# Normalisation statistics in four groups of eight tiles, with three of the roots on GpSimd, and parts and middle parts at other places in the order

## What is computed

```
xn = layernorm(x)                        # (x - mean) / sqrt(var + 1e-5)
Q, K, V = relu(xn @ W + b)               # 16 heads of 8 features
s  = softmax(causal(Q K^T / sqrt(8)), keys of live rows) V, masked by live queries
s  = gamma * norm(s + xn) + beta
# the other branch, on xn:
xa = (norm(xn) * ln_scale + ln_bias) @ attn_w.T + attn_b + xn
h  = gelu(xa @ w1[expert] + b1);  eo = h @ w2[expert] + b2
g  = silu(gelu(eo @ next_w.T + next_b))
out = x + s * g
```

## Time and profile before

| | us |
|---|---|
| three runs | 449.56, 454.50, 458.17 |
| median of the runs | 454.5 |
| the profiled execution, its own time | 449.74 |
| span of the profiled execution (first to last instruction) | 447.7 |
| mean granted TensorE clock, share of full | 0.977 |

### The profile page before, as it was taken

The page is one execution under the profiler, slowest core; times in us unless marked ns, Lnnn a source line. Parts: engine busy times, 40 slices in busy tenths (PEclk is TensorE's granted clock), DMA queues, the critical chain, the costliest instruction groups (busy, mean ns, idle before and its releaser), DMA issues.

```text
span 447.7 us, 9695 instructions
## 1 busy us (share of the span) xinstructions
PE 382.7 (85%) x3541; PEld 249.0 (56%) x3541; DVE 370.2 (83%) x865; ACT 289.1 (65%) x580; POOL 173.5 (39%) x448
## 2 busy tenths in 40 slices
PE   0046997899999996999999999999999999999950
PEld 0023863477777873466656665666566566656420
DVE  5899698968988523989899998999998998989427
ACT  0115742388888971377877877878778778778740
POOL 8333004211011122102147456556374474565591
PEclk9996899999999999999999999999999999999995
DMA  8930300386553428332332423332423324240000
GB/s 232 295 91 1 89 13 0 102 145 154 154 153 91 131 52 175 57 94 78 92 78 68 127 60 112 83 92 77 131 63 93 100 76 118 62 110 27 3 25 23
DMA packets 31413, 41.72 MB, mean 93 GB/s; under 512 B 5910, under 2 KB 23686, under 8 KB 31366
## 3 DMA queue, kind: packets, MB, share of 16 engines
q1 hardware_dynamic: 31206, 41.08, 35.3%
q0 software_dynamic: 160, 0.03, 0.1%
HBM read 26.43 MB, written 11.02 MB: 84 GB/s over the span
## 4 chain that ended last, share of the span: by engine, by line
PE 44%; DVE 13%; issue 2%; ACT 1%; POOL 1%; DVEq 0%; ACTq 0%; POOLq 0%
PE banks L1154 15%; PE banks L1137 8%; DVE mx L953 8%; PE banks L1117 8%; PE banks L1119 5%; PE banks L1139 5%; DVE stats L998 2%; PE banks L1164 2%; DVE res L992 1%; ACT pt L1072 1%; PE banks L1126 0%; DVE res L979 0%; DVE res L982 0%; DVE mixed L983 0%; DVE aggr L1002 0%
## 5 line engine op out<-in xcount | busy, mean ns | idle before, releaser
L953 DVE TENSOR_REDUCE mx<-banks 128x1 f32<-128x512 f32 (+3 forms) x352 | 200.1, 636 | 19.9 <-PE banks L1119 18.2
L1072 ACT ACTIVATE pt<-banks 128x512 f32<-128x512 f32 x320 | 169.2, 601 | 44.2 <-PE banks L1139 36.8
L1154 PE MATMUL banks<-pt,vg 128*18 128x512 f32 (+3 forms) x1024 | 81.4, 436 | 0.7 <-ACT pt L1072 0.7
L1117 PE MATMUL banks<-k_own,q_own 76*128 76x384 bf16 (+2 forms) x192 | 48.4, 274 | 5.5 <-DVE mx L953 2.7
L1117 PE MATMUL banks<-w_room 76*128 76x384 bf16 (+2 forms) x192 | 48.1, 274 | 3.3 <-DVE mx L953 3.3
L844 POOL TENSOR_SCALAR mneg<-mx 128x16 f32<-128x16 f32 x32 | 8.1, 253 | 108.1 <-DVE mx L953 106.9
L1137 PE MATMUL banks<-w_room 76*128 76x384 bf16 (+2 forms) x192 | 47.5, 275 | 0.9 <-ACT pt L1072 0.5
L1154 PEld LDWEIGHTS banks<-pt,vg 128*18 128x18 f32 x1024 | 23.7, 97 | 43.8 <-issue 33.4
L1137 PE MATMUL banks<-q_own,k_own 76*128 76x384 bf16 (+2 forms) x192 | 47.8, 274 | 0.0
L1119 PE MATMUL banks<-k_own,q_own 124*128 124x128 bf16 x256 | 44.0, 219 | 0.0
L1119 PE MATMUL banks<-w_room 124*128 124x128 bf16 x256 | 43.8, 219 | 0.0
(11 more groups left out here) (177 smaller groups left out, 746.7 us busy)
## 6 DMA issues: line engine op xcount, KB each, us to landing
k_scratch<-parts SPq DMA_DIRECT2D x40, 128.0 KB, 2.4
k_own<-k_scratch SPq DMA_DIRECT2D x48, 96.0 KB
w_room<-k_scratch SPq DMA_DIRECT2D x48, 96.0 KB
q_scratch<-parts SPq DMA_DIRECT2D x24, 128.0 KB, 2.4
q_own<-q_scratch SPq DMA_DIRECT2D x32, 96.0 KB
w_room<-q_scratch SPq DMA_DIRECT2D x32, 96.0 KB
w_room<-in_w_dram SPq DMA_DIRECT2D x1, 2048.0 KB, 9.3
q_own<-q_scratch SPq DMA_DIRECT2D x16, 112.0 KB
```

The costliest lines, as they stand in the source:

```text
L953: dve.tensor_reduce(mx[:, u % 2, heads[0]:heads[-1] + 1, q], banks[:, S0 + slots[0] % SLOTS, 0:w * len(heads)].rearrange("p (h k) -> p h k ...
L1072: act.activation(pt[:, T * j:T * j + T], banks[:, bank(), :], ACT.Exp, scale=SCALE).then_inc(exp_done, 1)
L1117: mm(o[:, 0:w - P], qx[by][0:LIVE, g, h, P * q:P * q + P], kx[by][0:LIVE, g, h, 0:w - P], start=True, stop=True)
L1154: ins = mm(banks[32 * h:32 * h + VP, OT, P * k:T], vg[:, g, k, h, :], pt[:, KPLACE[k, h]:KPLACE[k, h] + n], start=(k == 0 and g % 2 == 0), ...
```

## The change

The x rows are still loaded in two pieces (`LOADS`), but the statistics are made in four groups of eight tiles, one group for two sequences. The roots of group 0 stay on VectorE. For groups 1 to 3 VectorE makes means, variances and the seed (`statistics`, which increments `first_seeds`), GpSimd does the three Newton steps and the correction of the root (`first_roots`, 27 instructions) and, at a later place, its halves (`root_halves`, 4 instructions, then `roots_ready`), and VectorE takes the reciprocal (`inverses`) ahead of the quotients. `halves` splits by a product with 4097 in place of a mask of bits, since GpSimd does it in float32. The second roots are done for each of the four groups. On VectorE `sums(i)` stands right behind `quotients(i)`, then `lows(i - 2)`, then `rests(i - 1)`, and the statistics of groups 2 and 3 come behind these at i = 2 and i = 4; those of group 1 ahead of `quotients(1)`. On ScalarE both middle parts (`mids(i)`) move from between the gelus of h to behind the gelu of g in `gelu_out(i)`, for the last sequence behind its eight gelus; sequence 0 has another order, and a gelu of one element stands at the start. On TensorE the 68 held products at i = 1 go, and 22 stand at the start, behind waits for `bias_ready` and `seeds_ready`.

```diff
-GROUPS = ((0, 2 * TB), (2 * TB, NT - 2 * TB))
+LOADS = ((0, 2 * TB), (2 * TB, NT - 2 * TB))
+GROUPS = tuple((2 * TB * k, 2 * TB) for k in range(B // 2))
...
-HELD = (28, 40)
+HELD = 22
...
+                def halves(x, hi, lo, u, w):
+                    link(pool.tensor_scalar(u, x, 4097.0, None, ALU.mult))
+                    link(tt(w, u, x, ALU.subtract))
+                    link(tt(hi, u, w, ALU.subtract))
+                    link(tt(lo, x, hi, ALU.subtract))
+                def first_roots(tok, group):
+                    at = slice(group[0], group[0] + group[1])
+                    a_, y_, t_, u_, s_, sh_, sl_, rem_ = (v[:, at] for v in (a, y, t, t3, s, sh, sl, rem))
+                    pool.wait_ge(first_seeds, tok.next(first_seeds))
+                    for _ in range(3):
+                        link(tt(t_, y_, y_, ALU.mult))
+                        link(tt(t_, t_, a_, ALU.mult))
+                        link(pool.tensor_scalar(t_, t_, -0.5, 1.5, ALU.mult, ALU.add))
+                        link(tt(y_, y_, t_, ALU.mult))
+                    link(tt(s_, a_, y_, ALU.mult))
+                    halves(s_, sh_, sl_, t_, u_)
+                    link(tt(t_, sh_, sh_, ALU.mult))
+                    link(tt(rem_, a_, t_, ALU.subtract))
+                    link(tt(t_, sh_, sl_, ALU.mult))
+                    link(tt(t_, t_, t_, ALU.add))
+                    link(tt(rem_, rem_, t_, ALU.subtract))
+                    link(tt(t_, sl_, sl_, ALU.mult))
+                    link(tt(rem_, rem_, t_, ALU.subtract))
+                    link(tt(t_, rem_, y_, ALU.mult))
+                    link(pool.tensor_scalar(t_, t_, 0.5, None, ALU.mult))
+                    link(tt(s_, s_, t_, ALU.add))
+                def root_halves(group):
+                    at = slice(group[0], group[0] + group[1])
+                    halves(s[:, at], sh[:, at], sl[:, at], t[:, at], t3[:, at])
+                    pool.sem_inc(roots_ready, 1)
...
                 for i in range(B):
-                    if i == 0:
-                        second_roots(tok, GROUPS[0])
-                    if i == 2:
-                        second_roots(tok, GROUPS[1])
+                    if i % 2 == 0:
+                        second_roots(tok, GROUPS[i // 2])
                     totals(tok, i)
+                    if i % 2 == 1 and i + 1 < B:
+                        root_halves(GROUPS[(i + 1) // 2])
+                    if i % 2 == 0 and i + 2 < B:
+                        first_roots(tok, GROUPS[i // 2 + 1])
...
+                def inverses(tok, group):
+                    at = slice(group[0], group[0] + group[1])
+                    dve.wait_ge(roots_ready, tok.next(roots_ready))
+                    link(dve.reciprocal(r[:, at], s[:, at]))
+                    link(dve.tensor_scalar(nr[:, at], r[:, at], -1.0, None, ALU.mult))
...
+                def statistics(group):
+                    at = slice(group[0], group[0] + group[1])
+                    means(group)
+                    variances(group)
+                    rsqrt_newton(link, dve, y[:, at], t[:, at], a[:, at], 0)
+                    dve.sem_inc(first_seeds, 1)
                 tok = Tokens(dve)
                 dve.wait_ge(x_in[0], 16)
                 means(GROUPS[0])
                 variances(GROUPS[0])
                 roots(GROUPS[0])
-                quotients(0)
-                second_seeds(GROUPS[0])
-                sums(0)
-                quotients(1)
-                sums(1)
-                dve.wait_ge(x_in[1], 16)
-                rests(tok, 0)
-                means(GROUPS[1])
-                lows(tok, 0)
-                variances(GROUPS[1])
-                roots(GROUPS[1])
-                second_seeds(GROUPS[1])
-                rests(tok, 1)
-                for i in range(2, B):
+                for i in range(B):
+                    if i == 1:
+                        dve.wait_ge(x_in[1], 16)
+                        statistics(GROUPS[1])
+                    if i % 2 == 0:
+                        if i > 0:
+                            inverses(tok, GROUPS[i // 2])
+                        second_seeds(GROUPS[i // 2])
                     quotients(i)
-                    if i > 2:
+                    sums(i)
+                    if i > 1:
+                        lows(tok, i - 2)
+                    if i > 0:
                         rests(tok, i - 1)
-                    sums(i)
-                    lows(tok, i - 1)
+                    if i % 2 == 0 and 0 < i < B - 2:
+                        statistics(GROUPS[i // 2 + 1])
                 masks()
+                lows(tok, B - 2)
                 rests(tok, B - 1)
                 lows(tok, B - 1)
...
                     if i < B - 1:
+                        mids(tok, i)
                         product_out(tok)
 
-                def split(tok, i):
-                    for o, bias, done in ((0, bq, q_done), (1, bk, k_done)):
-                        act.wait_ge(done, tok.next(done))
-                        stored = parts_out[i % 2][o]
-                        act.wait_ge(stored, tok.next(stored, 16 * STORES[o]))
-                        act.activation(full[:, o, :], banks[:, QB + o, :], ACT.Relu, bias=bias)
-                        act.activation(parts[:, i % 2, o, 0, :], banks[:, QB + o, :], ACT.Relu,
-                                       bias=bias).then_inc(split_ready, 1)
+                def mids(tok, i):
+                    for o in range(2):
+                        act.wait_ge(rest_ready, tok.next(rest_ready))
+                        act.activation(parts[:, i % 2, o, 1, :], rest[:, o, :], ACT.Copy).then_inc(mid_ready, 1)
+                def split(tok, i, o):
+                    bias, done = ((bq, q_done), (bk, k_done))[o]
+                    act.wait_ge(done, tok.next(done))
+                    stored = parts_out[i % 2][o]
+                    act.wait_ge(stored, tok.next(stored, 16 * STORES[o]))
+                    act.activation(full[:, o, :], banks[:, QB + o, :], ACT.Relu, bias=bias)
+                    act.activation(parts[:, i % 2, o, 0, :], banks[:, QB + o, :], ACT.Relu,
+                                   bias=bias).then_inc(split_ready, 1)
...
+                def values_out(tok, i):
...
+                act.activation(hid[0:1, 0, 0, 0:1], ident[0:1, 0:1], ACT.Gelu)
                 norm_out(tok, 0)
-                split(tok, 0)
                 second_norm(tok, 0)
+                split(tok, 0, 0)
                 second_out(tok)
+                split(tok, 0, 1)
                 product_out(tok)
+                values_out(tok, 0)
                 for i in range(B):
                     n, last = i % STEPS, i == B - 1
                     if i > 0:
-                        split(tok, i)
+                        split(tok, i, 0)
+                        split(tok, i, 1)
+                        values_out(tok, i)
...
                         ins.then_inc(hid_ready, 1)
-                        act.wait_ge(rest_ready, tok.next(rest_ready))
-                        act.activation(parts[:, i % 2, h, 1, :], rest[:, h, :], ACT.Copy).then_inc(mid_ready, 1)
+                    if last:
+                        mids(tok, i)
...
-                    if i == 0:
-                        pe.wait_ge(bias_ready, 1)
...
+                pe.wait_ge(bias_ready, 1)
+                pe.wait_ge(seeds_ready, 1)
+                hold(HELD)
...
-                        if i == 1 and h == 1:
-                            hold(HELD[0])
...
-                    if i == 1:
-                        hold(HELD[1])
```

More of the change, by code:

```diff
@@ L218, in build_program @@
         TRX, TRL, QB, KB, VB, XB, H0B = range(7)
-        x_in = [sem(f"x_in{k}") for k in range(len(GROUPS))]
+        x_in = [sem(f"x_in{k}") for k in range(len(LOADS))]
         rows_in, bias_ready = sem("rows_in"), sem("bias_ready")
@@ L228, in build_program @@
         lanes_ready, seeds_ready = sem("lanes_ready"), sem("seeds_ready")
+        first_seeds, roots_ready = sem("first_seeds"), sem("roots_ready")
         xl_ready = sem("xl_ready")
@@ L243, in build_program @@
             "mask_ready", "maskT_done", "maskT_ready", "mask_out"))
-        mean, var, a, y, t, s, sh, sl, r, nr, rem, v2, y2, t2 = (small[:, k, :] for k in range(14))
+        mean, var, a, y, t, s, sh, sl, r, nr, rem, v2, y2, t2, t3 = (small[:, k, :] for k in range(15))
         with nc.Block() as block:
@@ L249, in _ @@
             def _(sp):
-                for k, (t0, n) in enumerate(GROUPS):
+                for k, (t0, n) in enumerate(LOADS):
                     sp.dma_start(x_all[:, t0:t0 + n, :], x_tiles[:, t0:t0 + n, :]).then_inc(x_in[k], 16)
@@ L294, in _ @@
                 pool.memset(q_fixed[:, 0, :], 1.0).then_inc(blank, 1)
-                for t in (ident, ident_b):
-                    pool.affine_select(out=t[:, :], in_=t[:, :], compare_op=ALU.not_equal, fill=1.0, base=0,
+                for unit in (ident, ident_b):
```

(1 more changed line is left out.)

## The result

| | before | after |
|---|---|---|
| four runs each, us | 458.17, 449.56, 454.50, 449.58 | 459.90, 460.20, 460.06, 460.06 |
| median, us | 452.04 | 460.06 |
| ratio of after to before, 95% interval | | 1.0196, 1.0116 to 1.0276 |
| span of the profiled execution, us | 447.7 | 458.2 |

The changed kernel is slower, by 8 us on the medians and by 10.5 us from one profiled span to the other. I had forecast no change, 452.0 us, with 459.0 as the upper end. The times of the kernel before fall into two groups (in the 65 runs taken beside the experiments 31 of 447.1 to 450.1 us and 34 of 454.5 to 459.5), while those of the changed kernel don't scatter; the experiments show that this is part of the answer.

A forecast was written before the change was run, and what follows sets the result against it. Stage one was taken as bound by VectorE before sequence 2, then TensorE; 449.74 - 1.6 (`second_normed(7)` earlier) + 1.55 (tail) = 449.7 us own time, named 452.0 half-way to the median, range 446 to 459.

The forecast's parts named there:

- the walk along VectorE: Stage one: adds VectorE's work and waits in order, letting `second_normed` of sequences 5, 6, 7 start at 123.1, 138.6, 151.1 us.
- GpSimd: Stage one: `first_roots` of 8.6 to 9.3 us just fits its 8.8 us cover; VectorE waits 2.1 us, then 1.3 twice.
- Rival 1: Stage one: GpSimd too slow, `first_roots` 13.0 us in place of 8.8, ending at 457 us own time; chance 0.12.
- the 0.48 us: Stage one: time of a linked GpSimd instruction while VectorE does `rests` and the three wide instructions of `quotients`.
- TensorE's clock in stage one: Clock falls in idle gaps of 6 to 7 us ahead of `second_normed` of 1, 3 and 5.
- The 0.7 us charged for the third: Clock fall ahead of `second_normed(5)` makes sequence 6 start at 139.3 us rather than 138.6.
- The tail: End of stage one: last middle part behind the second four gelus starts the SyncE store chain 1.55 us later.
- The price of a fall: Stage one: after a clock fall about 5 us run at half speed, costing 2.5 us.
- rival 2: Stage one, sequence 5: clock stays low through the whole sequence, some 13 us less slack, 461 us own; chance 0.03.
- Half of the distance to the median: Final sum: 452.0 us named half-way between 449.7 and the median of runs 449.56, 454.50 and 458.17.

The follow-up runs named there:

- experiment 10: Changed kernel with last middle parts back between the gelus, 19 idle products, plus 24 held products in each of stage one's three gaps: 448.97 us median.
- experiment 1: Changed kernel with 24 idle products in place of 10 at the end of stage one: 450.59 us median, ratio 1.0033 to the kernel before.
- experiment 2: Kernel before with 2 idle products in place of 10: 459.03 us, ratio 1.0217.
- experiment 4: Kernel before with only the last sequence's middle parts moved behind the second four gelus: 459.8 us median, ratio 1.0229.
- experiment 7: Changed kernel, 10 idle products, with fillers of 124 rows in place of 76 in stage two's first two units: 452.18 us median, ratio 1.0083.
- experiment 9: Kernel before with fillers of 124 rows in place of 76 in stage two's first two units: 450.14 us median.
- experiment 3: Changed kernel with the last sequence's middle parts back between the gelus: four of ten runs at 448.6 to 449.0 us, six at 456.8 to 458.9.
- experiment 5: Changed kernel with the last sequence's middle parts back between the gelus and 19 idle products in place of 10: 448.55 us median, ratio 0.9999.
- experiment 8: Changed kernel with last middle parts back between the gelus, 19 idle products and fillers of 124 rows in place of 76: 448.47 us median.
- experiment 6: Kernel before with 20 idle products in place of 10: 450.03 us median, seven of ten from 447.9 to 451.0, three from 457.4 to 459.5.

## Why the prediction was wrong

**What bounds the kernel, and the walk along VectorE: right.** 123.1 was forecast for `second_normed(5)` and 123.94 measured, 139.3 and 140.11 for 6, 153.0 and 153.59 for 7; waits on GpSimd were 0.4 to 0.5 us longer than taken, as `first_roots` ran past its cover. The gain ahead of sequence 2 (67.40 in place of 86.34) is spent on the statistics of groups 2 and 3, as said.

**GpSimd: mechanism right, a price misread.** It is disturbed by `rests`, `lows` and the wide three of `quotients`, hardly by the fours, beside which the instructions of `first_roots` came every 0.28 to 0.45 us. Rival 1 came only to its edge, with 9.6 us for the cover of 8.8. The Trainium skill ("GPSIMD Engine Reference", "Key points") says that GpSimd contends for SBUF with VectorE instructions with two SBUF inputs, as the fours have; the trace goes against it for them, here too. But the 0.48 us that I took beside `rests` and the wide three was a slip: between the rows at 70.62 and 74.44 lie six instructions and not eight, so it is 0.64. `totals(6)`, with `lows` and `rests` beside it, then took 3.9 / 6 = 0.65 each, and from the end of `sums(6)` to `second_normed(6)` were 5.9 us in place of 5.1.

**TensorE's clock in stage one: right in place, mis-sized in effect.** It fell in the three gaps of 5.9 to 6.6 us and was back 4.1 to 6.1 us after TensorE had resumed. The 0.7 us charged for the third was nothing (experiment 10): GpSimd's totals took that time anyway, so it is luck that the 139.3 came near the 140.11.

**The tail: this step failed.** I wrote that the chain of stores starts 1.55 us later, added 1.55 to the time and stopped there. What is late next was the question that I had set for every edit, and I had the numbers for the answer: TensorE's last product ends with its own list, which came 0.9 us earlier, while the boundary moved to 0.8 later, so its idle went from 2.6 to 4.3 us. I had used the fall of the clock some 4 us after the last product at the end of the kernel for the gaps of stage one, and had not asked it of the boundary. For the 2.6 us that the boundary already had, my one case was an idle of 2.09 us that left the clock high; the same trace holds the other case, an idle of 2.22 us behind which it fell, at 38.0, as the next products show (two of 128x512 take 1.02 us at the high clock):

```profile
37.31 0.66 PE L632 MATMUL banks<-ident,xl_st 128*128 128x128 f32 x4 [2.22 <-ACT xl_st L538]
38.84 2.08 PE L651 MATMUL banks<-xlT,wattn_sb 128*128 128x512 f32 x2 [0.87 <-ACT xlT L550]
```

The fall at the boundary costs 9.7 us (experiments 1, 2 and 4), far more than the 1 us that the change gained in stage one. The sum without it, 449.7, is close to what experiment 1 gave, 450.6; of the difference 0.3 is the tail's 1.85 in place of 1.55, and 0.6 the later `second_normed(7)`.

**The price of a fall was also wrong in kind.** I took 2.5 us from the w1 products of stage one. At the boundary it is 9.7, because the fillers of 76 rows there don't bring the clock back (experiment 7); my rival 2, a clock that stays low, stood at 0.03 and in the wrong stretch.

**The scatter of before was misread.** I took the 449.56 to 458.17 for noise around a middle and named a time between. It was this same fall, present in half of the runs (experiment 9). The changed kernel turned half of the runs into all of them. Half of the distance to the median, which I had added to the sum, was half of a fall, and no run of the changed kernel was near it. The Trainium skill ("TensorE: Matmul & The Clock Gate", "HAM oscillation") says that gaps in which TensorE waits for data bring the clock down; the trace agrees, at the boundary more than in the loop where I applied it.

## What to carry to other kernels

When a step at the end of a stage moves by a microsecond, compute how long TensorE idles across the boundary, and what runs behind it: a time that splits into two groups of runs, as 447 to 450 and 454 to 459 here, can be a sign that such a gap already stands at the edge. Set fillers so that they reach the next stage's start with the scatter of the store issues counted in, and give products that should bring back the clock many rows (here 124 did it and 76 did not). And an earlier start is worth only what reaches the last sequence: the statistics, now spread over stage one, made VectorE take 117.52 - 81.38 = 36.1 us for a pair of sequences against TensorE's 27.3, and of the 19 us won at sequence 2 about 1 was left at sequence 7.

## What the runs showed of the hardware that I had not expected

- How much idle TensorE's clock survives was not the same in each execution. In the 18 gaps of 5.9 us and more in the profiles of the changed kernel and of experiments 1, 3, 5, 7 and 8 it fell each time, 2.1 to 4.8 us after the last product. At the boundary, behind 4.2 to 4.5 us of idle, it was down in all four profiles, and by their times in all 16 runs of these four kernels. Behind 2.6 us it fell, by the times, in about half of the runs; where it did in a profile (experiment 3, 2.56 us) it fell 0.5 us after TensorE had started again, and behind 1.92 us (experiment 6) 0.6 us after. Behind 1.2 us two runs of ten were long in experiment 1 and none of ten in experiment 10 (1.26 us), behind 0.8 us none of ten (experiment 5).
- TensorE, busy without a gap, stayed at 1.2 GHz for 27 us, from 176.42 to 203.1, on score products of 76 and 124 rows and, up to 194.6, fillers of 76 rows and 512 columns. With fillers of 124 rows the clock rose 6 us after the start (experiment 7). In stage one of the changed kernel, on products of 128 rows, most of them float32, it took 4.1 to 6.1. At the high clock the same products of 76 rows did not let it fall (kernel before, experiments 1 and 5).
- In the five profiles with the long low stretch the clock rose 7 to 9 us after the last filler, and in three of them (experiments 2, 3 and 6) before the first float32 products of stage two. Experiment 3, where the products at 199.05 are already fast:

```profile
199.05 0.22 PE L1182 MATMUL banks<-k_own,q_own 76*128 76x128 bf16 x1
...
199.60 1.49 PE L1219 MATMUL banks<-pt,vg 128*18 128x512 f32 x16
```

  So the rise needs no float32 product; what the score products alone do, with no filler ahead of them, was not tried.
- Five store issues in SyncE's queue took 3.1 us in most places. On the last chain one profile of twelve had 4.6, which moved the start of stage two; on the chain of sequence 5 nine of twelve had 4.0 to 4.7.
